# Two stages of a graph layer in another order: GpSimd tells arrivals itself, ScalarE makes one-hots first, and the first projection signs each weight unit right after sizing it

## The reference

```
xn = (x - mean(x)) / sqrt(var(x) + 1e-5)
for l in range(2):
    q = (x @ Wq[l] + bq[l]).reshape(N, H, D)        # k, v alike; x is xn in layer 0
    a = (q[dst] * k[src]).sum(-1) / 8                # scores of 40000 edges
    e = exp(a - segment_max(a, dst)[dst])
    alpha = e / (segment_sum(e, dst)[dst] + 1e-16)
    agg = segment_sum(alpha[:, :, None] * v[src], dst).reshape(N, C)
    x = agg + (x @ Ws[l] + bs[l]) + enc
# then two layer norms round a feed-forward layer; beside it a slice attention of xn;
# last a gated feed-forward whose weights w are made ternary in groups of 128:
#   scale = mean(|w|) + 1e-5;  wq = clip(round(w / scale), -1, 1) * scale
```

## Time and profile before

| | us |
|---|---|
| median of three runs | 3154.48 (3148.83 to 3156.06) |
| the profiled execution: its time | 3161.87 |
| the profiled execution: its span | 3160.2 |
| first projection | 85 to 314 |
| edge attention, layer 0: scores, softmax, values | 314 to 760, to 805, to 1164 |
| second projection | 1164 to 1368 |
| edge attention, layer 1 | 1370 to 1813, to 1870, to 2220 |
| the rest, which the change leaves alone | 2220 to 3160 |

### The profile page before, as it was taken

The page is one execution under the profiler, slowest core; times in us unless marked ns, Lnnn a source line. Parts: engine busy times, 40 slices in busy tenths (PEclk is TensorE's granted clock), DMA queues, the critical chain, the costliest instruction groups (busy, mean ns, idle before and its releaser), DMA issues. The chain is left out here.

```text
span 3160.2 us, 50179 instructions
## 1 busy us (share of the span) xinstructions
PE 2531.4 (80%) x9914; PEld 1849.9 (59%) x9914; DVE 2163.0 (68%) x3476; ACT 1170.8 (37%) x4350; POOL 1648.5 (52%) x1559
## 2 busy tenths in 40 slices
PE   1888787765898779977877669888785999699998
PEld 1666444443775557744544358666564767477776
DVE  5776677878977666657877888677464454566665
ACT  0554566654000021136666610001353322155554
POOL 0111677777777741146767777777122443355555
PEclk8999788986899989988888779999887999899999
DMA  2666777776777776667777767777432332251110
GB/s 96 237 239 213 246 240 242 240 236 197 204 218 220 218 236 228 197 216 238 240 242 239 221 185 214 213 224 221 150 134 93 106 121 93 98 167 41 40 46 33
DMA packets 244253, 575.14 MB, mean 182 GB/s; under 512 B 32642, under 2 KB 70894, under 8 KB 242834
## 3 DMA queue, kind: packets, MB, share of 16 engines
q0 software_dynamic: 100160, 328.28, 35.8%
q1 hardware_dynamic: 126546, 212.27, 19.7%
q10 hardware_dynamic: 17280, 31.63, 2.7%
HBM read 465.00 MB, written 107.06 MB: 181 GB/s over the span
## 5 line engine op out<-in xcount | busy, mean ns | idle before, releaser
L1357 POOL DMA_INDIRECT edge_ring<-k_rows,edges_src x626 | 592.7, 947 | 282.3 <-issue 135.9
L1357 POOL DMA_INDIRECT edge_ring<-v_rows,edges_src x626 | 617.2, 986 | 223.5 <-issue 140.6
L1666 PE MATMUL edge_psA<-layer_q_space 128*128 128x256 f32 (+1 forms) x2656 | 628.9, 392 | 95.3 <-DVE layer_q_space L1490 87.8
L1666 PEld LDWEIGHTS edge_psA<-layer_q_space 128*128 128x128 f32 x2656 | 495.5, 192 | 228.4 <-issue 159.2
L1490 DVE TENSOR_TENSOR layer_q_space<-edge_ring,edge_psQ 128x512 f32<-128x512 f32 x664 | 426.6, 683 | 162.1 <-SPq L1275 133.1
L1413 DVE TENSOR_TENSOR edge_ring<-edge_psQ,edge_ring 128x512 f32<-128x512 f32 x532 | 346.9, 682 | 175.5 <-ACT edge_ring L1502 71.6
L1502 ACT ACTIVATE edge_ring<-edge_ring 128x64 f32<-128x64 f32 x1328 | 320.1, 242 | 285.9 <-DVE edge_ring L1413 285.9
L1619 PE MATMUL edge_psQ<-layer_q_space,edge_hotT 128*128 x1064 | 363.3, 474 | 15.9 <-DVE edge_ring L1413 13.3
L108 PE MATMUL proj_psP<-proj_w,proj_xT 128*128 128x512 f32 x1440 | 354.9, 403 | 6.5 <-DVE proj_xT L866 4.0
L108 PEld LDWEIGHTS proj_psP<-proj_w,proj_xT 128*128 128x128 f32 x1440 | 270.8, 191 | 68.8 <-DVE proj_xT L866 4.4
L1394 DVE TENSOR_REDUCE layer_scores<-edge_ring 128x24 f32<-128x1536 f32 x166 | 289.1, 1742 | 0.0
(11 more groups left out here) (309 smaller groups left out, 3625.8 us busy)
## 6 DMA issues: line engine op xcount, KB each, us to landing
v_xT<-proj_xT SPq DMA_DIRECT2D x40, 512.0 KB, 4.9
edge_x_halves<-v_xT SPq DMA_DIRECT2D x80, 256.0 KB, 5.4
agg_rows<-layer_q_space ACTq DMA_DIRECT2D x40, 260.0 KB, 3.6
base_rows<-proj_enc SPq DMA_DIRECT2D x40, 256.0 KB, 2.0
k_rows<-proj_out ACTq DMA_DIRECT2D x40, 256.0 KB, 3.8
v_rows<-edge_ring ACTq DMA_DIRECT2D x40, 256.0 KB
edge_ring<-k_rows,edges_src POOLq DMA_INDIRECT x626, 4.0
edge_ring<-v_rows,edges_src POOLq DMA_INDIRECT x626, 3.8
```

The costliest lines, as they stand in the source:

```text
L1357: pool.indirect_dma_start(ring[:, buffer[n], :], None, rows, bass.IndirectOffsetOnAxis(ap=T["src"][:, t:t + 1], axis=0)).then_inc(landed[b ...
L1666: last = pe.matmul(psA[:, bass.ds(d % 2, 1), e, 0:hi - lo].rearrange("p o w -> p (o w)"), hot[:, s % R, :], wv[:, s % R, lo:hi], start=Fal ...
```

## The change

There are three parts. In the first projection, x gets four buffers and two places for statistics; the statistics and the root of a tile are made three tiles ahead, the scaling stays two ahead; ScalarE sizes and signs a unit before it goes to the next, and both before it takes the units of the tile before; VectorE goes by unit too, and does the Q part last. In the scores, ScalarE makes the one-hots of a batch before it sums up the fourth slot of the batch two before. In the arrivals, GpSimd waits for the landing of gather n - 4 as it did, and tells the arrival itself; SP, which no longer waits for landings, goes through releases, row loads and half loads sorted by slot.

```diff
-        layer, XB = 0, 3
+        layer, XB = 0, 4
...
-        ln = LayerNorm(nc, m, 1)
+        ln = LayerNorm(nc, m, 2)
...
-                ln.root(act, 0)
-                ln.root(act, 1)
...
+                root(0)
+                root(1)
+                root(2)
                 for i in range(4 * KC):
                     act.copy(w[:, 0, i, :], T["w_rows"][:, i, :]).then_inc(w_highs, 1)
...
                 for i in range(NT):
                     if i + 1 < NT:
                         high(i + 1)
+                    for u in units(i):
+                        size(u)
+                        sign(u)
                     if i:
                         q_part(i - 1)
-                    if i + 2 < NT:
-                        ln.root(act, i + 2)
-                    for u in units(i):
-                        size(u)
                     for u in units(i - 1):
                         take(u)
+                    if i + 3 < NT:
+                        root(i + 3)
                     act.wait_ge(ready, i * 3 + K_ + 1)
                     act.dma_start(k_dram[i * P:(i + 1) * P, :], out[:, i % 2, :]).then_inc(k_out[i % 2], 16)
-                    for u in units(i):
-                        sign(u)
...
-                normalise(0)
-                normalise(1)
+                stats(0)
+                apply(0)
+                stats(1)
+                apply(1)
+                stats(2)
...
                     if i + 2 < NT:
-                        normalise(i + 2)
-                    if i:
-                        q_less(i - 1)
+                        apply(i + 2)
+                    if i + 3 < NT:
+                        stats(i + 3)
                     add(i, S_)
                     add(i, K_)
                     for u in units(i):
                         size_up(u)
-                    for u in units(i):
                         choose(u)
-                    add(i, Q_)
+                    if i:
+                        q_less(i - 1)
                     for u in units(i - 1):
                         low_unit(u)
+                    add(i, Q_)
...
+                def done_in(h):
+
+                    i, half = divmod(h, 2)
+                    return V_AT[i] + 1 + half
+
+                load_rows(0)
+                load_rows(1)
+                sp.wait_ge(k_arrived, K_FIRST + 1)
...
+                in_turn = [(r + 16, release, (r, multiplied)) for r in range(ET - 3)]
+                for k in range(2, -(-USED // PER_ROWS)):
+                    in_turn.append((k * PER_ROWS - 12, load_rows, (k,)))
+                for h in range(XH, 2 * NT):
+                    in_turn.append((done_in(h - XH) * B, load_half, (h,)))
+                for _slot, do, what in sorted(in_turn, key=lambda x: x[0]):
+                    do(*what)
...
+                def arrive(n):
+
+                    pool.wait_ge(*landing[n])
+                    pool.sem_inc(k_arrived if n < ET else v_arrived, 1)
+
                 def gather(n, rows, t):
-                    if n >= FLIGHT:
-
-                        pool.wait_ge(*landing[n - FLIGHT])
...
                 for t in range(ET):
+                    if t >= FLIGHT:
+                        arrive(t - FLIGHT)
                     if t >= NB:


                         pool.wait_ge(k_released, t - NB + 1)
-                        pool.sem_inc(started, 1)
                     gather(t, k_dram, t)
...
                 for j in range(BATCHES):
-                    if j >= 2:
-                        reduce(j - 2)
                     act.wait_ge(spread, j + 1)
...
                     act.activation(hotT[j % 2], apart[:, j % 2, :], ACT.Relu, bias=1.0, scale=-1.0
                                    ).then_inc(hotT_ready, 1)
+                    if j >= 2:
+                        reduce(j - 2)
```

More of the change, by code:

```diff
@@ L623, in normalise_project @@
         out = m.sb("out", [P, 2, C])
-        bias_parts = m.sb("bias_parts", [1, 2, C], F32R)
+        bias_parts = T["q_parts"][0:1, 0, NT - 2:NT, :]
         qsum = m.sb("qsum", [P, C])
@@ L820, in take, with root @@
                     act.copy(mag[:, u % RAW], psW[u % 2][:]).then_inc(taken, 1)
-                ln.root(act, 0)
-                ln.root(act, 1)
+                def root(i):
+                    if i == 0:
+                        act.wait_ge(ln.have_eps, 1)
+                    act.wait_ge(ln.have_mv, i + 1)
+                    act.activation(ln.std[:, i % 2:i % 2 + 1], ln.mv[:, i % 2, 1:2], ACT.Sqrt,
+                                   bias=ln.eps[:, 0:1]).then_inc(ln.have_std, 1)
+                root(0)
+                root(1)
+                root(2)
                 for i in range(4 * KC):
@@ L831, in q_part @@
                     act.wait_ge(ready, i * 3 + Q_ + 1)
+                    if i == NT - 2:
+                        act.wait_ge(v_parts_out, 32)
                     act.copy(qp[:, 0, i, :], qsum[:]).then_inc(rounded, 1)
@@ L854, in _, with stats, apply @@
             def _(vec):
-                def normalise(i):
+                def stats(i):
                     vec.wait_ge(x_in[i % XB], i // XB * 16 + 16)
+                    vec.bn_stats(ln.st[:, i % 2, :], x[:, i % XB, :]).then_inc(ln.have_st, 1)
+                    vec.wait_ge(ln.have_st, i + 1)
+                    vec.bn_aggr(ln.mv[:, i % 2, :], ln.st[:, i % 2, :]).then_inc(ln.have_mv, 1)
+                def apply(i):
+                    vec.wait_ge(ln.have_std, i + 1)
                     if i:
                         vec.wait_ge(normed, i)
-                    ln.stats(vec, lambda n: x[:, i % XB, :], i)
-                    ln.scale(vec, i)
-                    ln.apply(vec, 0, x[:, i % XB, :], x[:, i % XB, :]).then_inc(normed, 1)
+                    vec.reciprocal(ln.rstd[:, i % 2:i % 2 + 1], ln.std[:, i % 2:i % 2 + 1]).then_inc(ln.have_rstd, 1)
+                    vec.wait_ge(ln.have_rstd, i + 1)
+                    vec.wait_ge(ln.have_mv, i + 1)
+                    ln.apply(vec, i % 2, x[:, i % XB, :], x[:, i % XB, :]).then_inc(normed, 1)
                 def low(i):
@@ L1251, in edge_attention @@
         rows_in = [m.sem(f"rows_in{half}") for half in range(2)]
-        started, reduced_act, lifted, topped, spread, hotT_ready, queried, multiplied, reduced, distant, padded = (
-            m.sem(x) for x in ("started", "reduced_act", "lifted", "topped", "spread", "hotT_ready", "queried", "multiplied", "reduced", "distant", "padded"))
+        reduced_act, lifted, topped, spread, hotT_ready, queried, multiplied, reduced, distant, padded = (
+            m.sem(x) for x in ("reduced_act", "lifted", "topped", "spread", "hotT_ready", "queried", "multiplied", "reduced", "distant", "padded"))
         nearby, turned, in_rows, steps, ends_done, ends_in, best_done, best_out, ready, exped, returned, stored = (
@@ L1272, in _ @@
             def _(sp):
-                def arrive(n, signal):
-                    sp.wait_ge(*landing[n])
-                    sp.sem_inc(signal, 1)
                 ends_of = {}
                 def release(r, used):
-                    if r < 0:
-                        return
                     if r // B not in ends_of:
@@ L1296, in load_half, with load_rows @@
                                      :, :, half * 2 * P:(half + 1) * 2 * P]).then_inc(half_in[h % XH], 16)
[L1298 to L1309, removed]
+                def load_rows(k):
                     n = min(PER_ROWS, USED - k * PER_ROWS)
@@ L1316, in _ @@
                                  ).then_inc(rows_in[k % 2], 16)
[L1317 to L1333, removed]
+                def done_in(h):
[4 more added lines that the diff above has]
+                sp.wait_ge(k_arrived, K_FIRST + 1)
+                sp.dma_start(wv_parts.rearrange("p h k c -> p (h k c)"), later_v["w"]).then_inc(wv_in, 16)
+                sp.dma_start(bias_rows, later_v["bias"].rearrange("o (h c) -> (o h) c", h=2)).then_inc(wv_in, 16)
+                for h in range(XH):
+                    load_half(h)
+                in_turn = [(r + 16, release, (r, multiplied)) for r in range(ET - 3)]
[5 more added lines that the diff above has]
+                    do(*what)
                 sp.wait_ge(queried, USED)
@@ L1342, in _ @@
                 sp.wait_ge(stored, len(parts))
[L1343 to L1347, removed]
+                for r in range(ET - NV):
+                    release(r, weighted)
             @block.gpsimd
@@ L1359, in gather @@
                                             ).then_inc(landed[buffer[n]], 16)
+                pool.sem_inc(k_arrived, K_FIRST - 1)
+                pool.sem_inc(v_arrived, V_FIRST - 1)
                 for t in range(ET):
+                    if t >= FLIGHT:
+                        arrive(t - FLIGHT)
                     if t >= NB:
                         pool.wait_ge(k_released, t - NB + 1)
-                        pool.sem_inc(started, 1)
                     gather(t, k_dram, t)
-                pool.wait_ge(v_stored, 16 * NT)
```

(6 more changed lines are left out.)

1 line of the change is left out of this document (removed).

## The result

The changed kernel takes 3206.89 us (median of 4 runs, 3201.35 to 3209.76) against 3153.72 for the kernel before: a ratio of 1.0169, 95% interval 1.015 to 1.0187, or 53 us slower. Forecast were 3131 us, and the range ended at 3160. The forecast was wrong in sign, and none of the three rivals names what happened.

What follows compares the result with a forecast made beforehand. GpSimd's chain of gathers was taken to bound the edge stages. Half loads -21.7, first projection -4 and its start +2.2 gave -23.5 us: 3138.4 from the profiled 3161.87, 3131 on the median's footing; range 3098 to 3160.

Steps and rivals of the forecast that it cites:

- three rivals: Alternatives to the forecast: more gained, around 3105 us (0.12); nothing gained, 3149 to 3160 (0.19); slower, 3167 (0.15).
- Arrivals by GpSimd: Edge gathers: GpSimd already waits for the landing, one signal replaces another, step stays at 1.25 us: 0.
- The room of a gather: Edge gathers: 5.0 us before a gather holds up the fourth behind it; median 3.9, about 1.1 left.
- Half loads one at a time: Loads of x during K gathers: 37 singles a layer at 0.25 us replace pairs and singles, 21.7 us gained.
- the prices: K gathers' loss to loads of x: a pair costs 1.4 to 1.6 us, a single 0.25.
- signature of 405 to 412: Trace sign: K gathers of a layer span 405 to 412 us rather than 420.
- One-hots first: ScalarE's order in the scores: VectorE's waits may shift or shrink, but lie beside the gathers: 0.
- the signature given for it: Trace sign in the scores: VectorE's waits for ScalarE shrink, from 43.0 us in layer 0.
- First projection: Loop of weight units: 0.9 us gained per three tiles, 4 us in all, less 2.2 lost at its start.
- The late start: Start of the first projection: weight casts begin at about 85.8 instead of 83.64, 2.2 us lost.
- the second, costs by bytes: Rival on half loads: cost follows bytes in flight, 0.45 to 0.65 us a half, nothing gained, 3149 to 3160; chance 0.19.
- The third: Rival on half loads: a single costs half a pair or more, 0.74 us, so slower, 3167; chance 0.15.

Runs made afterwards that it cites:

- True pairs: Changed kernel with the landing waited for by the gather itself and two half loads issued in the same microsecond, 18 pairs a layer: 3142.59 us, ratio 0.9996.

## Why the prediction was wrong, step by step

**The step that failed** is "Arrivals by GpSimd ... one signal takes the place of another (`started`), so the step stays at 1.25: 0". The free step did stay at 1.25. But the two waits of GpSimd changed places: the landing was waited for by the gather, and is waited for now by the signal ahead of it, and the gather waits for the release, which in the changed kernel's trace comes 9 us or more before each K gather that needs it. So GpSimd does not wait "as it did", as the section on the change has it. That is worth 57 us by the medians (3206.9 to 3149.4) and 64 by the ratios (1.0169 to 0.9967) when it is moved back, and 56 or 61 when it is put into the old kernel, and turns a gain into the loss. The prediction counted instructions and not which of them carried the binding wait.

The diff shows it: `pool.wait_ge(*landing[n - FLIGHT])` leaves `gather` and stands in `arrive` with a signal behind it. The Trainium skill, "Perfetto Trace Analysis", has a possible reason, in the sections "Sequencer-only Instruction (DRAIN, etc)" and "DMA Instruction — SWDGE (GPSIMD)": an instruction of the sequencer alone waits in the sequencer, which takes up the next one only afterwards, while an indirect DMA is taken up, put into a queue and waits there. The profile lists these signals among the sequencer's instructions (POOLq). The traces agree as far as they go: 0.26 us from landing to start when the gather waits, 0.77 when the signal does. The page gives no figure for it; what happens within the 0.51 us no view here shows.

**The room of a gather** was given as 5.0 us. It was 4.75 before, since a held gather starts 0.26 after the landing. In the changed kernel it is 4.24, near the median landing of 3.9, so more gathers come late as well: behind the first 30 K and the first 45 V gathers of a layer, 109 steps longer than 1.4 us in both layers together became 143.

**Half loads one at a time**, 21.7 us of gain, was mis-sized. In the traces pairs and singles hold the gathers alike, 22.6 and 22.1 us in layer 0, and by the ratios pairs cost 9 or 16 us where the prices give them 36; 256 KB more right behind a half cost 0.5 to 0.73 us, which is twice the 0.25 that the prediction has for a single half, or more, and well under the 1.4 less 0.25 that by its prices makes a pair of one. That the trace of before showed pairs at 1.4 and a single at 0.16 is true of it, but those singles stood a good 10 us from other halves, and the new ones 4 to 9 us from the other half of their tile; that this distance makes the difference is likely and not shown. The rule of the Trainium skill that the prediction weighed ("DMA: Bandwidth & Descriptors", "Queues, rings and completion order") is that queues are served by turns. By it, as the prediction read it, splitting gains nothing; that lies nearer to the runs than 21.7 us, and they leave it open whether it is quite nothing. SP's list as a whole still gave 7 us (3 to 12). In its trace K gathers take 412.3 and 413.1 us, 7 less a layer than before, as the prediction's signature of 405 to 412 nearly had it; some of that is lost again in the stretches between and after the layers, which took 8 us longer in this trace. True pairs reach the same K gathers, which speaks against the splitting as the reason. Which part of the list does it, the later or steadier times of the halves or the releases, was not tried.

**One-hots first** was taken as 0; 4 us faster with no change within the interval. That holds. VectorE waited no less for ScalarE, so the signature given for it was wrong (before 43.0 us). For arrivals it waits longer in the changed kernel; the line of before stands first:

```profile
DVE edge_ring L1413 <- SPq L1275: 29.8, 7, 11.1
...
DVE edge_ring L1425 <- POOLq L1360: 48.3, 13, 12.3
DVE edge_ring L1425 <- ACT edge_ring L1514: 46.9, 34, 2.9
```

In the run with the one-hots alone none of this shows in the time.

**First projection.** Its sum was -2 us, measured -6 (-2 to -11) in the kernel by itself. Single traces can't tell more: the first K gather starts between 308.5 and 313.7 us in the eight with the new order, and between 310.7 and 313.9 in the five with the old. In the changed kernel's trace ten tiles from the flip at 173.51 take 115.4 us, before 118.2 (from 173.95 to 292.12): 0.8 for three tiles where 0.9 was forecast.

```profile
173.51 0.60 PE L750 MATMUL proj_psT<-kept_ident,proj_x 128*128 128x128 f32 x4
...
288.95 0.60 PE L750 MATMUL proj_psT<-kept_ident,proj_x 128*128 128x128 f32 x4
```

The late start is there too, with the casts at 85.29 (before 83.64, forecast 85.8):

```profile
85.29 2.16 ACT L833 CAST proj_w<-layer_q_space 128x512 fp32r<-128x512 f32 x4
```

**Of the rivals** the second, costs by bytes, comes nearest for the halves. The third had the right sign for another reason, and nothing in it would have led to GpSimd's queue.

## What to carry to other kernels

Where an engine's chain of waits and issues sets the time, let the instruction that matters carry the wait that comes last, and put the waits that are long satisfied, and the signals, ahead of it; look in a diff for which instruction holds which wait before counting instructions. Where a transfer is held by the landing of one n before it, compare the room with the spread of landings, not with their median: here two more gathers in flight were worth 78 us in the old kernel, more than seven times what all parts of the change gave together with the wait in its place (10), and took the cost of the misplaced wait away as well. What a trace shows of two cases that differ in distance and in amount (pairs, and singles far from others) is not yet the price of either.

## What the runs showed of the hardware that was not expected

A GpSimd instruction that only waits and signals, placed ahead of an indirect DMA, makes a held DMA start 0.77 us after the landing that it waits for (the changed kernel, and the one before with the waits swapped); with the wait on the DMA itself it is 0.26 us (the kernel before, and the changed one with the wait on the gather). Medians and, for K gathers, both quartiles are the same. Indirect gathers of 128 rows of 2 KB run at one in 1.25 us with six in flight, next to 256 KB loads from another queue. The median landing of layer 0's K gathers then takes 3.96 us in place of 3.92 in the kernel before, 4.17 in place of 3.91 in the changed one, and 4.29 in place of 4.14 with the wait on the gather: two more transfers in flight lengthen the single landing a little, and the chain of gathers gets shorter all the same.
